# Loading joined with the first similarity, the last similarity begun inside the kernel mix, and rows of inverse lengths moved four at a time

## The chip, the cores and the metric

The kernel runs on one core of a Trainium2 chip. The core has a matrix engine (TensorE, PE in the rows; PEld is its loading of stationary operands), three engines for elementwise work (VectorE, DVE; ScalarE, ACT; GpSimd, POOL), a queue that issues transfers (SyncE, SP) and 16 DMA engines that share them. Each engine runs its own list of instructions in order and waits on semaphores that others raise. The metric is the device time of one execution in microseconds (us), measured over several runs.

## The reference, cut to what matters

`x` is 64 batches of 128 x 512 values, `adj` is 128 x 128. Four layers follow one another, each with a residual sum and a normalisation over the last axis. Layers 0 and 3 are alike and are the ones touched:

```python
def _ada_gcn(xn, weight, bias):             # xn: 512 x 64 x 128
    x_norm = xn / jnp.maximum(jnp.linalg.norm(xn, axis=-1, keepdims=True), 1e-12)
    mean_sim = jnp.einsum('nbl,mbl->nm', x_norm, x_norm) / B
    _, idx = jax.lax.top_k(mean_sim, k + 1)  # k = 153; the row itself is left out
    ...                                      # A: the kept similarities, An: A scaled by its degrees
    xw = jnp.einsum('nbl,lo->nbo', xn, weight)
    return jnp.einsum('sd,sbl->dbl', An, xw) + bias
x = _layernorm(x + _L0_gnn_ref(x, adj, L0_gnn_bias), axis=-1)
x = _layernorm(x + _L1_gnn_ref(...))         # mixes the 128 tokens, adj as kernel
x = _layernorm(x + _L2_gnn_ref(...))         # two causal kernels per batch, made from x
x = _layernorm(x + _L3_gnn_ref(x, adj, L3_gnn_bias), axis=-1)
```

The mean similarity is a sum over all 64 batches of 512 x 512 Gram matrices of columns scaled to length one. So a layer's similarity needs, for every batch, its 512 inverse column lengths, and the choice of neighbours can begin only when all 64 batches are summed.

## The kernel before, in words

All of `x` stays on the chip as `X`, 128 partitions by 64 batches by 512. The stages, each closed by a barrier of all engines, are: `load_x`; `select_neighbours` for layer 0, which is `similarity` and then `neighbours`; `propagate_and_mix_tokens` (layers 0 and 1); `kernel_mix` (layer 2, 16 groups of four batches in a software pipeline); `select_neighbours` for layer 3; `propagate` with the stores of the output.

**Inverse lengths.** In layer 0 ScalarE squares each batch (L448) and TensorE sums the squares over partitions into one row of a bank `rows_bank` (L459). Even and odd batches and the two halves of `x` go to bands of this bank. `ColumnScales` turns the rows into inverse lengths: `clamp` and the maximum (L198, L200), a root on ScalarE, `invert` (L208), `refine` (L213 to L217), and `store` writes them to memory outside the core as `rn_rows` (L222). It exists twice per layer: `early` for the rows that are done when the stage before ends (half of the batches in layer 0, all but the last `LATE` groups in layer 3) and `late` for the others, whose inverse is computed between groups of the similarity.

**Similarity.** For batch b, SyncE brings row b of `rn_rows`, spread over all partitions (256 KB), into slot r = b mod 4 of `rnb` (L514), as soon as the multiply of batch b - 4 has read that slot. VectorE multiplies `X[b]` by it (L576, `unit`), ScalarE makes its 16-bit high part (L617, `hi`), VectorE subtracts to get the low part (L582, `lo`), and TensorE adds 11 products of high and low parts into four banks `pair` and one bank `diag` (L546 to L550). VectorE's list has four multiplies, then four subtractions, per group of four batches; the buffers `unit`, `hi` and `lo` hold four slots each. GpSimd only stores the late rows and takes the greatest of the squared lengths over partitions (L537), which VectorE needs at the end for the scaled weights (L602 to L607). In layer 3, `LastGroup` normalises the last four batches and takes their squares during the first groups.

**Kernel mix.** Step s of the pipeline projects and compares group s, finishes group s - 1 (turned kernels L1748, masks and sums L1913 to L1952, outputs L1979 into `X`, moments, normalising L1819) and takes the squares and sums of group s - 2 (L1803, L2030, L1733). Step 16 has no new group, only what is left of the last two; behind it, `early` of layer 3 stores its rows (L222) and the stage ends.

What sets the order is the order of the code for each engine, written by hand, with semaphore counts between engines.

## Time and profile before

| | |
|---|---|
| median of 3 runs | 1421.34 us (1420.53 to 1422.23) |
| profiled execution | 1420.99 us, its span 1419.3 us |
| mean granted TensorE clock | 0.966 of full speed |
| TensorE busy | 1313.2 us, 93% of the span |
| weight loads (PEld) | 726.5 us, 51% |
| VectorE busy | 1081.6 us, 76% |
| ScalarE busy | 818.8 us, 58% |
| GpSimd busy | 566.3 us, 40% |

The stages in the trace: loading to 60 us, the first similarity to 167.8, neighbours and propagation behind it, the kernel mix to some 1060, the second similarity to 1170, then neighbours, propagation and the stores of the output. A row of the timeline is a run of like instructions: start, time from the first's start to the last's end, engine, line, output and inputs, size, and in brackets how long the engine sat idle before it and what released it. The landing time of a transfer runs from its issue to its last byte.

### The profile page before, as it was taken

To read this page: it belongs to the slowest core of one execution; us is meant where nothing else is said; L and a number is where in the kernel's file an instruction comes from. 1 tells how busy PE (TensorE), PEld (TensorE's weight loads), DVE (VectorE), ACT (ScalarE), POOL (GpSimd) and SP (SyncE) were. 2 spreads that over 40 slices of the span, in tenths; PEclk is the share of its full clock that TensorE was granted. 3 is DMA by queue.
4 is the path that set the end of the run, shared out by engine and by line. 5 is a ranking of instruction groups with operands and counts; after the bars stand their busy time and mean duration, and the time that the engine had idled before them with its cause. 6 is when DMAs were issued, how large, how long until landed. Compare 5 with 4: busy or idle time off the path is not lost. (4 is left out here: it accounts for less than half of the span.)

```text
span 1419.3 us, 29584 instructions
## 1 busy us (share of the span) xinstructions
PE 1313.2 (93%) x8776; PEld 726.5 (51%) x8806; DVE 1081.6 (76%) x2169; ACT 818.8 (58%) x1366; POOL 566.3 (40%) x866
## 2 busy tenths in 40 slices
PE   6689988999999889999999999999947997999997
PEld 2156555555555345555555555555514567455553
DVE  0498777888888847888888888888788988356664
ACT  5634345787777633555555555555445446477776
POOL 2100114787787711222222222222222001688887
PEclk9999987999999889999999999999988998999999
DMA  8756200000000022112211111222205440122222
GB/s 325 266 189 210 89 0 1 1 0 0 0 0 0 12 49 38 38 38 38 38 37 37 37 37 37 43 39 39 36 13 177 161 136 1 45 90 81 81 81 97
DMA packets 122971, 93.62 MB, mean 66 GB/s; under 512 B 87712, under 2 KB 87840, under 8 KB 122912
## 3 DMA queue, kind: packets, MB, share of 16 engines
q1 hardware_dynamic: 122720, 92.81, 22.7%
q8 instruction: 31, 0.51, 0.1%
q14 instruction: 28, 0.23, 0.0%
q0 software_dynamic: 192, 0.08, 0.0%
HBM read 54.86 MB, written 17.04 MB: 51 GB/s over the span
## 5 line engine op out<-in xcount | busy, mean ns | idle before, releaser
L546 PE MATMUL pair<-unit_lo,unit_hi 128*128 128x512 f16 x512 | 178.8, 386 | 29.5 <-ACT unit_hi L617 24.7
L2030 POOL TENSOR_TENSOR sq_lo<-sq,sq_hi 128x512 f16<-128x512 f32 x60 | 69.6, 1160 | 139.2 <-ACT sq_hi L1803 139.2
L550 PE MATMUL diag<-unit_hi 128*128 128x128 f16 x512 | 113.4, 221 | 0.0
L548 PE MATMUL pair<-unit_hi 128*128 128x384 f16 (+2 forms) x384 | 106.4, 277 | 0.0
L1150 PE MATMUL po<-an_h,xwh 128*128 128x512 f16 x256 | 98.0, 383 | 0.0
L1151 PE MATMUL po<-an_l,xwh 128*128 128x512 f16 x256 | 97.9, 382 | 0.0
L1152 PE MATMUL po<-an_h,xwl 128*128 128x512 f16 x256 | 97.8, 382 | 0.0
L1785 PE MATMUL work<-m_h,xT 128*128 128x512 f16 x256 | 97.0, 379 | 0.0
L1786 PE MATMUL work<-m_l,xT 128*128 128x512 f16 x256 | 97.0, 379 | 0.0
L1787 PE MATMUL work<-m_h,xT 128*128 128x512 f16 x256 | 97.0, 379 | 0.0
L1089 POOL TENSOR_TENSOR x_all<-x_all,t 128x512 f32 (+1 forms) x64 | 81.2, 1269 | 16.8 <-ACT t L983 12.1
L2047 POOL TENSOR_TENSOR rnl<-rnl,scalars 128x4 f32<-128x4 f32 x16 | 16.6, 1035 | 176.2 <-DVE rnl L1991 176.2
L1334 POOL TENSOR_TENSOR x_all<-x_all,t 128x512 f32 (+1 forms) x64 | 81.2, 1269 | 9.1 <-ACT t L1235 5.1
L546 PEld LDWEIGHTS pair<-unit_lo,unit_hi 128*128 128x128 f16 x512 | 50.8, 99 | 58.4 <-DVE unit_lo L582 34.0
L550 PEld LDWEIGHTS diag<-unit_hi 128*128 128x128 f16 x512 | 50.9, 99 | 47.2 <-issue 3.3
L617 ACT ACTIVATE unit_hi<-xT 128x512 f16<-128x512 f32 x64 | 39.7, 630 | 60.9 <-DVE xT L576 33.9
L617 ACT ACTIVATE unit_hi<-kept 128x512 f16<-128x512 f32 x64 | 39.3, 628 | 59.6 <-DVE kept L576 37.6
L1870 ACT ACTIVATE v_h<-work 128x512 f16<-128x512 f32 x48 | 28.7, 597 | 77.5 <-PE work L1787 77.5
L1376 PE MATMUL po<-an_h,xwh 128*128 128x512 f16 x184 | 69.7, 379 | 0.0
L1377 PE MATMUL po<-an_l,xwh 128*128 128x512 f16 x184 | 69.7, 379 | 0.0
L1378 PE MATMUL po<-an_h,xwl 128*128 128x512 f16 x184 | 69.7, 379 | 0.0
L1105 POOL TENSOR_TENSOR rstd<-rstd,scalars 128x2 f32<-128x2 f32 (+1 forms) x67 | 65.5, 978 | 10.1 <-POOL rstd L1103 8.6
(438 smaller groups left out, 4237.7 us busy)
## 6 DMA issues: line engine op xcount, KB each, us to landing
x_all<-in_x_dram SPq DMA_DIRECT2D x16, 1024.0 KB, 14.5
tl<-rn_rows SPq DMA_DIRECT2D x64, 256.0 KB, 3.7
sim<-rn_rows SPq DMA_DIRECT2D x64, 256.0 KB, 3.7
out_dram<-x_all SPq DMA_DIRECT2D x64, 256.0 KB, 2.0
weights_a<-in_L_gnn_W_lang_dram SPq DMA_DIRECT2D x1, 1024.0 KB, 11.4
weights_b<-in_L_gnn_W_grav_dram SPq DMA_DIRECT2D x1, 1024.0 KB, 8.3
weights_a<-in_L_gnn_W_O_dram SPq DMA_DIRECT2D x1, 1024.0 KB, 10.6
an_h<-in_L_gnn_W_V_dram SPq DMA_DIRECT2D x1, 512.0 KB, 5.6
```

The source lines that it names most:

```text
L546: nc.tensor.matmul(pair[i][:], stat, lo[:, r, :], start=first, stop=False, skip_group_check=True)
L548: nc.tensor.matmul(pair[i][:, (i + 1) * P:], stat, hi[:, r, (i + 1) * P:], start=False, stop=final, skip_group_check=True)
L550: last = nc.tensor.matmul(diag[:, i * P:(i + 1) * P], stat, stat, start=(first and i == 0), stop=final, skip_group_check=True)
L617: nc.scalar.activation(hi[:, r, :], unit[:, r, :], ACT.Copy).then_inc(hi_ready, 1)
L1089: pool.tensor_tensor(X[:, b, :], X[:, b, :], t[:, r, :], ALU.add).then_inc(add_r, 1)
L1150: nc.tensor.matmul(po[r][:], wh[:, r, cs], an_h[:, c, :], start=(c == 0), stop=False)
L1151: nc.tensor.matmul(po[r][:], wh[:, r, cs], an_l[:, c, :], start=False, stop=False)
L1152: last = nc.tensor.matmul(po[r][:], wl[:, r, cs], an_h[:, c, :], start=False, stop=(c == C - 1))
L1334: pool.tensor_tensor(X[:, b, :], X[:, b, :], t[:, r, :], ALU.add).then_inc(add_r, 1)
L1785: nc.tensor.matmul(work[j][:], xT_h[:, j, d, :], w["m_h"][:, d, :], start=(d == 0), stop=False)
L1786: nc.tensor.matmul(work[j][:], xT_h[:, j, d, :], w["m_l"][:, d, :], start=False, stop=False)
L1787: last = nc.tensor.matmul(work[j][:], xT_l[:, j, d, :], w["m_h"][:, d, :], start=False, stop=(d == C - 1))
```

## The change

- `load_x` and `similarity` of layer 0 become one stage, `load_and_compare`; the barrier between them is gone.
- The similarity of layer 3 is begun in step 16 of the kernel mix (`closing`), whose list for each engine is now written out: groups of the similarity stand between pieces of the mix's last two groups. The clamp, inversion and refinement of the early rows, the first four multiplies and high parts move into step 15. `LATE` goes from 2 to 3 groups. The mix's own banks `work0` to `work3` and `gram_l` are the similarity's `pair` and `diag`; their names stay in the rows.
- One transfer of four rows (1 MB) fills all four slots of the one buffer `rnb`; it is issued when all four multiplies of the group before are done.
- The low parts of slots 1 and 3 are made by GpSimd, in both layers.
- From the seventh sixteenth of `x` on, GpSimd squares one batch in four.
- GpSimd's reduction of the greatest squared length stands at the end of its list, behind its last subtraction. Weight transfers are issued later and in smaller pieces.

```diff
-LATE = 2
+LATE = 3
+class Similarity:
+    R = 4
...
+    def load(self, sp, base):
+        if not isinstance(base, int) or base > 0:
+            settle(sp, self.unit_ready, base, self.k.idle["sp"])
+        row = base if self.layer == 0 else B - self.R - base
+        sp.dma_start(self.rnb, self.k.rn_rows[bass.ds(row, self.R)].partition_broadcast(P)).then_inc(self.rn_in, 16)
...
+    def take_unit(self, dve, base, r, start=False):
+        b = base + r
+        dve.wait_ge(self.rn_in, (base // self.R + 1) * 16)
+        if not start:
+            dve.wait_ge(self.hi_ready, b - self.R + 1)
+            dve.wait_ge(self.lo_of(r), self.lo_count(base - self.R, r))
+        self.k.nc.vector.tensor_tensor(self.unit[:, r, :], self.k.X[:, b, :], self.rnb[:, r, :],
+                                       ALU.mult).then_inc(self.unit_ready, 1)
...
+    def units(self, dve, base, start=False):
+        for r in range(self.R):
+            self.take_unit(dve, base, r, start)
+        for r in range(0, self.R, 2 if self.shared else 1):
+            self.lo_on_vector(dve, base, r, start)
+
+    def lo_on_pool(self, pool, base, start=False):
+        for r in range(1, self.R, 2):
+            b = base + r
+            if not start:
+                settle(pool, self.gram_done, b - self.R + 1, self.k.idle["pool"])
+            settle(pool, self.hi_ready, b + 1, self.k.idle["pool"])
+            pool.tensor_tensor(self.lo[:, r, :], self.unit[:, r, :], self.hi[:, r, :],
+                               ALU.subtract).then_inc(self.lo_of(r), 2 if self.shared else 1)
...
-def load_x(k, x, adj, b0, b3, gate, logsig, mix, rows_bank, tiles, tokens):
+def load_and_compare(k, ctx_out, x, adj, b0, b3, gate, logsig, mix, rows_bank, ops, tokens):
...
                 early.store(sp)
                 early.all_stored(sp)
+                for base in range(0, B // 2, R):
+                    sim.load(sp, base)
+                    if base == 2 * R:
+                        sp.wait_ge(mix.lang.lo_r, C)
+                    if 2 * R <= base < 6 * R:
+                        mix.load_rows(sp, "wo", mix.a, base // R - 2)
+                sim.late.all_stored(sp)
...
                 mix.lang.lo_part(pool, mix.a)
+                for base in range(0, 3 * R, R):
+                    sim.lo_on_pool(pool, base, base == 0)
+                sim.late.store(pool)
+                with strided(pool, 3 * R, B, R) as base:
+                    sim.lo_on_pool(pool, base)
+                pool.wait_ge(early.top, 1)
+                sim.greatest(pool)
...
-def kernel_mix(k, w, rows_bank, head):
+def kernel_mix(k, w, rows_bank, head, work, pgl, pgg, ahead):
...
+                def closing():
+                    early.store(sp)
+                    early.all_stored(sp)
+                    sp.wait_ge(early.top, 1)
+                    for q in range(5):
+                        sim.load(sp, q * R)
+                    turn_kernels(NG - 1)
+                    for q in range(5, (B - LATE * G) // R):
+                        sim.load(sp, q * R)
+                    sim.late.store(sp)
+                    sim.late.all_stored(sp)
+                    for q in range((B - LATE * G) // R, B // R):
+                        sim.load(sp, q * R)
...
+                def closing():
+                    flips(NG - 1)
+                    pe.wait_ge(v_l, NG * G)
+                    pe.wait_ge(ksm, (NG - 1) * SMALL + 1)
+                    for r in range(R):
+                        sim.gram(pe, 0, r, r == 0, False)
...
+                def closing():
+                    ks = Kernels(NG - 1)
+                    for r in range(0, R, 2):
+                        sim.lo_on_vector(dve, 0, r, True)
+                    ks.add_turned()
+                    sim.units(dve, R)
+                    ks.mask_gravity()
+                    ks.sums()
+                    sim.units(dve, 2 * R)
+                    ks.factors()
+                    ks.mix()
...
+                        if before_close(s, 1):
+                            dve.wait_ge(gl_d, NG)
+                            dve.wait_ge(ln_r, (NG - LATE) * G)
+                            for r in range(R):
+                                sim.take_unit(dve, 0, r, True)
```

How the lists change. SyncE where the loading ends and the first similarity begins, before (`tl` is the buffer of the rows of inverse lengths, `an_l` the early inverse lengths):

```order
L222 DMA rn_rows<-an_l 16x512 x2
L394 UNCONDITIONAL_BRANCH
L508 UNCONDITIONAL_BRANCH
L514 DMA tl<-rn_rows 128x512 x4
L352 DMA weights_b<-in_L_gnn_W_grav_dram 128x4x512
L352 DMA weights_a<-in_L_gnn_W_O_dram 128x4x512
L57 UNCONDITIONAL_BRANCH
L57 ISA
L514 ISA
L514 DMA tl<-rn_rows 128x512
```

SyncE at the same place after:

```order
L223 DMA rn_rows<-an_l 16x512 x2
L410 DMA tl<-rn_rows 128x2048 x3
L356 DMA weights_a<-in_L_gnn_W_O_dram 128x512
L410 DMA tl<-rn_rows 128x2048
L356 DMA weights_a<-in_L_gnn_W_O_dram 128x512
L410 DMA tl<-rn_rows 128x2048
L356 DMA weights_a<-in_L_gnn_W_O_dram 128x512
L410 DMA tl<-rn_rows 128x2048
L356 DMA weights_a<-in_L_gnn_W_O_dram 128x512
L410 DMA tl<-rn_rows 128x2048 x2
```

Four row transfers have become one of four rows, the two large weight transfers have left this place, and one of them comes back in quarters.

GpSimd from the end of its weight work to the end of the first similarity, before (`wl_l` is the low part of a weight, L537 the reduction):

```order
L314 TENSOR_TENSOR wl_l<-weights_a,wl_h 128x128
L394 UNCONDITIONAL_BRANCH
L148 ISA
L530 UNCONDITIONAL_BRANCH
L222 DMA rn_rows<-an_l 16x512 x2
L537 ISA
L537 ISA scalars<-scalars 128x1
L507 UNCONDITIONAL_BRANCH
```

GpSimd over the same stretch after (L441 is `lo_on_pool`, L471 the reduction):

```order
L315 TENSOR_TENSOR wl_l<-weights_a,wl_h 128x128
L441 TENSOR_TENSOR unit_lo<-xT_18,unit_hi 128x512 x6
L223 DMA rn_rows<-an_l 16x512 x2
L57 UNCONDITIONAL_BRANCH
L57 ISA
L65 REGISTER_ALU
L441 TENSOR_TENSOR unit_lo<-xT_18,unit_hi 128x512
L65 REGISTER_ALU
L441 TENSOR_TENSOR unit_lo<-xT_18,unit_hi 128x512
L57 REGISTER_ALU
L57 COMPARE_AND_BRANCH
L471 ISA
L471 ISA scalars<-scalars 128x1
```

Two subtractions a group have come to GpSimd, and the reduction has moved from the middle of the stage to behind the loop of them.

VectorE at the end of the kernel mix, before (L1913 to L1932 are masks and sums of the last group):

```order
L1893 SCALAR_TENSOR_TENSOR v_l<-work_288,v_h 128x512
L1913 TENSOR_TENSOR gs<-gs,gram_l 128x512
L1915 TENSOR_TENSOR es<-es,gram_g 128x512
L1917 SCALAR_TENSOR_TENSOR gs<-gs,bcast 128x512
L1924 SCALAR_TENSOR_TENSOR es<-es,mask 128x512
L1930 TENSOR_REDUCE small<-gs 128x4
L1932 TENSOR_REDUCE small<-es 128x4
```

VectorE at the same place after (L418 is the multiply, L426 the subtraction of the similarity; `degrees` here is the bank that was `gram_g`, `diag` the one that was `gram_l`):

```order
L418 TENSOR_TENSOR tl<-x_all,xT_18 128x512 x4
L2014 SCALAR_TENSOR_TENSOR v_l<-work_217,v_h 128x512
L2014 SCALAR_TENSOR_TENSOR v_l<-work_218,v_h 128x512
L2014 SCALAR_TENSOR_TENSOR v_l<-work_219,v_h 128x512
L2014 SCALAR_TENSOR_TENSOR v_l<-work_220,v_h 128x512
L426 TENSOR_TENSOR tg_l<-tl,tg_h 128x512 x2
L2039 TENSOR_TENSOR gs<-gs,diag 128x512
L2041 TENSOR_TENSOR es<-es,degrees 128x512
L2043 SCALAR_TENSOR_TENSOR gs<-gs,bcast 128x512
L418 TENSOR_TENSOR tl<-x_all,xT_18 128x512 x4
L426 TENSOR_TENSOR tg_l<-tl,tg_h 128x512 x2
```

The multiplies of the first batches have come in front of the value parts of the last group, and the second group of the similarity stands between the last group's turned kernels and its sums.

## Rows read from the trace of the kernel before

**Rows 1.** Windows: stretch, length; busy (instructions) PE, PEld, DVE, ACT, POOL; clock, DMA, GB/s

```profile
102.00:166.00 64.00, 63.54 (x496) 38.84 (x494) 54.69 (x91) 26.89 (x44) 0.00 (x0) 1.00 0.56 180
1044.00:1048.00 4.00, 0.00 (x0) 0.00 (x0) 3.83 (x12) 1.44 (x3) 2.27 (x3) 0.52 0.00 0
```

**Rows 2.** Timeline, TensorE and ScalarE: start, length, engine, line, operation [idle before, releaser]

```profile
47.43 12.48 PE L459 MATMUL rows_bank<-sq,unit_col 128*32 128x512 f32 x46
69.72 0.61 PE L546 MATMUL pair<-unit_lo,unit_hi 128*128 128x512 f16 x1 [9.81 <-ACT unit_hi L617]
...
167.78 1.09 ACT L681 ACTIVATE xT<-pair 128x512 f32<-128x512 f32 x2 [4.21 <-PEq L507]
...
1040.26 0.60 PE L1748 MATMUL gram_g<-ident,es 128*128 128x128 f32 x4
1069.94 0.61 PE L546 MATMUL pair<-unit_lo,unit_hi 128*128 128x512 f16 x1 [10.48 <-ACT unit_hi L617]
...
1169.96 1.09 ACT L681 ACTIVATE kept<-pair 128x512 f32<-128x512 f32 x2 [4.21 <-PEq L507]
```

**Rows 3.** Timeline, VectorE, middle of the first similarity

```profile
151.99 2.50 DVE L576 TENSOR_TENSOR xT<-x_all,tl 128x512 f32<-128x512 f32 x4
157.64 2.50 DVE L576 TENSOR_TENSOR xT<-x_all,tl 128x512 f32<-128x512 f32 x4
```

**Rows 4.** Landing times: rows of layer 0 (L514), then parts of x (L400)

```profile
DMA to landing us min/median/max: 3.0/3.7/9.4
...
DMA to landing us min/median/max: 5.2/14.5/16.1
```

**Rows 5.** DMA view and timeline, 0 to 72 us

```profile
GB/s 0 232 379 34 116 313 407 396 387 387 389 387 386 386 390 386 386 383 393 386 385 385 391 387 388 382 391 386 348 161 13 0 0 0 110 341 221 283 385 413
...
tl<-rn_rows SPq DMA_DIRECT2D x8, 256.0 KB, 6.6
...
rn_rows<-an_l SPq DMA_DIRECT2D x2, 32.0 KB, 2.6
...
46.24 12.57 ACT L448 ACTIVATE sq<-x_all 128x512 f32<-128x512 f32 x24
...
51.89 0.82 SPq L222 DMA_DIRECT2D rn_rows<-an_l  x2
...
64.08 2.16 DVE L576 TENSOR_TENSOR xT<-x_all,tl 128x512 f32<-128x512 f32 x3 [9.07 <-DMA tl<-rn_rows]
...
65.01 4.62 SPq L514 DMA_DIRECT2D tl<-rn_rows  x4
```

**Rows 6.** Timeline, a subtraction on GpSimd beside VectorE's multiplies

```profile
1091.31 4.42 DVE L576 TENSOR_TENSOR kept<-x_all,sim 128x512 f32<-128x512 f32 x4
1091.94 3.24 POOL L1532 TENSOR_TENSOR early_xwl<-early_xwh 128x512 f16<-128x512 f32 x2 [7.79 <-ACT early_xwh L1527]
```

**Rows 7.** Timeline: reciprocal of the early rows, the reduction, the weights' chain

```profile
46.37 3.34 DVE L208 RECIPROCAL an_l<-an_h 64x512 f32<-64x512 f32 x1 [4.65 <-ACT an_h L204]
...
98.62 0.47 POOL L537 PARTITION_ALL_REDUCE scalars<-scalars  x1 [7.02 <-issue]
...
163.19 0.15 DVE L602 TENSOR_SCALAR scalars<-scalars 128x1 f32<-128x1 f32 x1
164.16 0.15 DVE L607 TENSOR_SCALAR scalars<-scalars 128x1 f32<-128x1 f32 x1
```

**Rows 8.** Timeline, last step of the mix

```profile
1026.16 2.73 DVE L1979 SCALAR_TENSOR_TENSOR x_all<-work,scalars,x_all 128x512 f32<-128x512 f32 x4 [4.16 <-PE work L1777]
...
1038.96 2.92 ACT L1819 ACTIVATE x_all<-x_all,rs 128x512 f32<-128x512 f32 x4
...
1047.03 1.81 DVE L1947 TENSOR_SCALAR gs<-gs,small 128x128 f32<-128x128 f32 x4
...
1059.06 1.68 SPq L222 DMA_DIRECT2D rn_rows<-xT  x4
```

More of the change, by code:

```diff
@@ L467, in _ @@
                         mix.lang.sum_squares(pe)
+                pe.wait_ge(mix.lang.tmp_r, C)
+                pe.wait_ge(mix.lang.q_in, 1)
+                for r in range(R):
+                    sim.gram(pe, 0, r, r == 0, False)
+                with strided(pe, R, B - R, R) as base:
+                    sim.grams(pe, base)
+                sim.grams(pe, B - R, True)
             @block.vector
@@ L640, in similarity @@
+                sim.units(dve, 0, True)
+                dve.wait_ge(sums, B)
+                sim.late.clamp(dve)
+                sim.units(dve, R)
+                sim.late.invert(dve)
+                sim.units(dve, 2 * R)
+                sim.late.refine(dve)
+                with strided(dve, 3 * R, B, R) as base:
+                    sim.units(dve, base)
+                sim.weights(dve)
     return pair, diag
@@ L1739, in _, with flips, flip @@
                 pe.wait_ge(msk_r, 2)
+                def flips(g):
+                    def flip(bank, src):
+                        for j in range(G):
+                            js = slice(j * P, (j + 1) * P)
+                            end = nc.tensor.transpose(bank[:, js], src[:, js], k.ident[:])
+                        return end
+                    pe.wait_ge(tl_c, g + 1)
+                    pe.wait_ge(diag_r, g * DIAG + 1)
+                    flip(pgl, gs)
+                    need(pe, sum_r, g)
+                    pe.wait_ge(dd_r, g + 1)
+                    nc.tensor.matmul(pbc[:], k.ones[:], dd[:], start=True, stop=True).then_inc(bc_d, 1)
+                    pe.wait_ge(tg_c, g + 1)
+                    flip(pgg, es).then_inc(bc_d, 1)
@@ new lines, in step @@
+                def step(s):
+                    if closes(s):
+                        return closing()
+                    if before_close(s, 1):
+                        dve.wait_ge(ns_d, (NG - LATE) * G)
+                        dve.wait_ge(v_d, (NG - 1) * G)
+                        dve.wait_ge(cleared, 1)
+                        early.clamp(dve)
+                    if s.live(1):
+                        ks = Kernels(s.at(1))
+                        ks.add_turned()
+                    if s.live(0):
+                        for e in range(2):
+                            lo(tl_lo[:, e, :], work[e][:], tl_hi[:, e, :], S_EVAC, tl_h, s.at(0) * C + e + 1, tl_l)
+                    if s.live(1):
+                        ks.mask_gravity()
+                    if s.live(0):
+                        lo(tl_lo[:, 2, :], work[2][:], tl_hi[:, 2, :], S_EVAC, tl_h, s.at(0) * C + 3, tl_l)
+                    if s.live(1):
+                        ks.sums()
+                    if s.live(0):
+                        lo(tl_lo[:, 3, :], work[3][:], tl_hi[:, 3, :], S_EVAC, tl_h, s.at(0) * C + 4, tl_l)
+                    if s.live(1):
+                        ks.factors()
+                        ks.mix()
@@ new lines, in closing @@
+                def closing():
+                    sim.lo_on_pool(pool, 0, True)
+                    mask_language(NG - 1)
+                    last.mark(pool)
+                    for q in range(1, 5):
+                        sim.lo_on_pool(pool, q * R)
+                    scales(NG - 2)
+                    choose(NG - 2)
+                    sim.lo_on_pool(pool, 5 * R)
+                    for j in range(G):
+                        square_lo(NG - 2, j)
+                    sim.lo_on_pool(pool, 6 * R)
+                    last.scales(pool)
+                    sim.lo_on_pool(pool, 7 * R)
+                    last.low_parts(pool)
+                    for q in range(8, B // R):
+                        sim.lo_on_pool(pool, q * R)
+                    sim.greatest(pool)
```

628 lines of the change are left out of this document (332 added, 296 removed).

## The prediction

> **What bounds the kernel now.** I read the page's slices of the span first: TensorE is 93% busy, and its bad slices lie where stages meet. The windows around two of these meetings come next. In the middle of the first similarity TensorE is busy 63.54 of 64.00 us at the full clock; at the end of the mix it does nothing in 1044 to 1048, and the granted clock is down at 0.52 there, the lower level of 1.2 GHz [rows 1]. The timeline gives the size. Join 1: the last square sums end at 59.9, the first Gram matmul starts at 69.72. Join 2: the last turned kernels leave at 1040.86, the first Gram matmul starts at 1069.94; only 12 output products and 8 sums lie between. Behind similarity 1 the next block starts at 167.78, behind similarity 2 at 1169.96, each as soon as TensorE is done [rows 2]. What the change can win is therefore at most some 10 us in join 1 and some 25 in join 2.
>
> In the steady part the four multiplies of one group start 5.65 us after those of the group before (151.99, 157.64) [rows 3]. That is TensorE's pace, 1.41 us a batch, since it never rests there [rows 1]. VectorE spends 2.50 on the multiplies of a group and as much on its low parts, so it has 0.65 us to spare.
>
> **The rows of inverse lengths: the term that decides.** Before, a 256 KB transfer brings one row into one of four slots, and it is issued as soon as that slot's multiply is done. It lands 3.7 us later in the median, 3.0 at best [rows 4]; with a multiply of 0.7 (three in 2.16 [rows 5]) that closes a loop of 4.6 per slot, shorter than 5.65, so it hides. After, one 1 MB transfer fills all four slots, and `load` waits for `unit_ready` of all four. There is no second buffer. So the loop is serial: four multiplies 2.50 [rows 3], the queue's reaction 0.2 (the first multiply of 64.08 is over at 64.80, its reload starts at 65.01) [rows 5], the landing, and 0.1 until VectorE starts.
>
> The landing of 1 MB is not seen alone for these rows; the nearest row is the load of x, same size, whose first transfer found an idle ring: 5.2 us, the least of its 16 [rows 4]. Bounds: 3.7, if size cost nothing, and 6.6, the median landing of the first eight quarter transfers, which shared the ring with 2 MB of weights [rows 5]. I take 5.2. The loop is 2.50 + 0.2 + 5.2 + 0.1 = 8.0 us for four batches instead of 5.65. TensorE then works 5.66 of 8.0 and waits the rest.
>
> The Trainium skill, DMA: Bandwidth & Descriptors, section Anatomy of one DMA, gives about 2.0 us plus bytes over 436 GB/s, which for 1 MB would be 4.4 us. The trace does not quite agree: its 256 KB need 3.0 at best where the rule has 2.6, and the lone 1 MB needed 5.2. By the rule the loop would be 7.2 and the sum near 1439; it is a rival below.
>
> **Half of the low parts on GpSimd.** Two of four subtractions per group leave VectorE (saving 1.2 us) for GpSimd. They don't come free: while GpSimd did two such subtractions in 3.24 us , VectorE's four multiplies took 4.42 instead of 2.50 [rows 3, 6]; I price it at 0.9 us of VectorE per GpSimd subtraction, nothing to 1.0 as bounds. That makes 6 x 0.62 + 2 x 0.9 = 5.5 per group against 5.0 before. In a loop of 8.0 this lies in the landing, so it costs nothing; with the old loop it would have been close to the bound.
>
> **Join 1.** The squares: GpSimd takes one in four from part 6 on, ScalarE's 0.52 per square (24 in 12.57 [rows 5]) was TensorE's wait, so the last 24 take 6 x 0.52 = 3 us less; nothing waits for that but the late rows. The early rows are refined earlier too, but their store stands in the same queue behind x, so I leave it landed at 52.3 + 2.6 = 54.9 [rows 5] (bound: 3 earlier). The load now follows at once, not behind a barrier and beside weights: issued 55.1, landed 60.3, first multiply 60.3 instead of 64.08, first Gram near 64 instead of 69.72. Then 15 loops: 60.3 + 15 x 8.0 = 180.3 for the last group's multiplies; 0.7 more for the 3.34 us reciprocal [rows 7] and the refinement, which stand between groups and mostly fall into landings. From there 2.50 multiplies, 1.1 to the first low parts, 4 x 1.41 Gram: TensorE ends at 190.3.
>
> Then the tail. `greatest`, the reduction over partitions, was done in the middle of the block (7.02 us in which GpSimd waits for no semaphore that the trace shows, then 0.47: 7.5 us) [rows 7]. Now it stands behind GpSimd's last subtraction. That one ends near 181.0 + 5.5; plus 7.5 and VectorE's five small steps, 163.19 to 164.31 or 1.1 [rows 7], gives 195.1, where TensorE was done at 190.3. With 0.3 to the next block: 195.4 against 167.78. **Join 1: +27.6.**
>
> **Join 2.** In step 15 the clamp lies under the turning of the kernels and the reciprocal in VectorE's idle 4.16 us before the outputs [rows 8]; the refinement delays it by about 2, and the moments of step 14 (3.3) have left. So rows are ready near 1029, four stores (1.68 us of issue [rows 8] and 2.6 to land [rows 5]) by 1033.3, the load by 1038.7. VectorE blocks there till its multiplies end at 1041.3, ScalarE puts four high parts between the value copies, and the values are complete near 1044; low parts and the first sum follow, the first Gram starts near 1046, 24 us earlier than now. That is the gain.
>
> The second group's load is issued at 1041.5, multiplies at 1047.2 behind the turned kernels. Then 14 loops of 8.0: 1159.2. VectorE's work of the last step (masks, sums, the 2.9 us of mixing that begins at 1047.03 [rows 8], moments, outputs; 26 us in all) mostly falls into landings. Not all: ScalarE's high parts of group 5 stand behind the normalising of step 14 (2.92 [rows 8]), which waits for GpSimd and the moments, 3.8 late; those of group 7 behind the last group's normalising and squares, 1.8; mixing and reciprocal 1.5; the stores of the late rows between loads 12 and 13, 1.3. Sum 8.4: last multiplies 1167.6, TensorE's end + 9.3 = 1176.9, tail as in join 1 + 4.8, plus 0.9 for three more steps, 0.3: 1182.9 against 1169.96. **Join 2: +12.9**: the 24 won are spent on 14 x 2.35 = 33 of loop.
>
> **Sum.** The profiled execution took 1420.99 us (span 1419.3; the median of the runs, 1421.34, is 0.35 above it). 1420.99 + 27.6 + 12.9 = 1461.5, so about **1462**, slower.
>
> **Rivals.**
> (a) The rule's landing of 4.4, loop 7.2: 15 x 0.8 and 14 x 0.8 less, 12.0 + 11.2, of which VectorE's crowded closing takes back some: near 1439. For it: the ring moved 385 to 413 GB/s through the load of x [rows 5], so a megabyte needs 2.7 of transfer, and a group's four rows are 8 KB in one piece. Against: the lone megabyte took 5.2. 0.22.
> (b) Loop longer than 8: GpSimd's subtractions meet the multiplies, or TensorE, idle a third of each loop, falls to the low clock. In join 2 the clock was down within 3 to 7 us after TensorE's last turn at 1040.86 [rows 1, 2]; the gaps here are 2.4. One more us of loop is 29 us: about 1490. 0.12.
> (c) The other side: faster. If a megabyte lands in 3.7 like a quarter of it, the loop is 6.5. Join 1 then costs 27.6 - 22.5 - 1.5 (first load) = 3.6; join 2, there bound by VectorE at (16 x 5.5 + 26) / 16 = 7.1 a group, wins 12.9 - 14 x 0.9 - 1.5 - 6 (ScalarE's late parts no longer the wait) = -7. Near 1418. It decides from a loop of about 6.6 down. Against it: 1 MB in the 1.4 us that a landing of 3.7 leaves is 750 GB/s, twice what x's load got [rows 5]. 0.07.
> (d) The joins don't overlap as told (a wait in step 15 that I missed holds the first Gram beyond 1050): 1470, inside the forecast's range.
> Forecast 0.59, with its own range 1450 to 1476.
>
> A measurement of this kernel tells 0.2%, some 3 us, from no change. Faster 0.06, same 0.03, slower 0.91. Range 1435 to 1484: it leaves out (c), half of (b) and the low edge of (a).
>
> **What would show it.** In the profile after: multiplies of one group start 7.5 to 8.5 us after the last group's, with VectorE's idle before them ended by the DMA of the rows; landings of these 1 MB transfers near 5.2; TensorE busy about 0.7 in both similarities at clock 1.00; first Gram near 64 and 24 us earlier in join 2; GpSimd idle 7 us before the reduction at each block's end, and VectorE waiting for it. I am wrong if the groups keep 5.7, if landings are below 4, or if the similarities are bound by VectorE or GpSimd rather than by the rows.

## The result, and the profile after

The changed kernel takes 1459.82 us in the median of four runs (1459.64 to 1463.21) against 1420.93 of before in the same session: ratio 1.028, 95% interval 1.0268 to 1.0293. It is slower by 39 us. Its profiled span is 1461.5 us against 1419.3.

| | before | after |
|---|---|---|
| span of the profiled execution | 1419.3 | 1461.5 |
| TensorE busy | 1313.2 (93%) | 1329.4 (91%) |
| VectorE busy | 1081.6 (76%) | 1089.4 (75%) |
| GpSimd busy | 566.3 (40%) | 666.1 (46%) |
| clock | 0.966 | 0.96 |

The middle of the first similarity, the stretch of [rows 1], in the windows after (same columns):

```profile
102.00:166.00 64.00, 47.25 (x358) 27.59 (x356) 47.33 (x51) 20.10 (x34) 25.09 (x18) 1.00 0.48 168
```

TensorE issues 358 matmuls where it issued 496, at the same clock, and is idle a quarter of the time. VectorE's timeline at the place of [rows 3], then SyncE's, then the landing times of the transfers of layer 0 and of layer 3 (from issue to last byte):

```profile
146.03 2.50 DVE L418 TENSOR_TENSOR xT<-x_all,tl 128x512 f32<-128x512 f32 x4 [2.14 <-DMA tl<-rn_rows]
148.44 3.20 DVE L426 TENSOR_TENSOR unit_lo<-xT,unit_hi 128x512 f16<-128x512 f32 x2
153.80 2.50 DVE L418 TENSOR_TENSOR xT<-x_all,tl 128x512 f32<-128x512 f32 x4 [2.16 <-DMA tl<-rn_rows]
...
148.75 8.12 SPq L410 DMA_DIRECT2D tl<-rn_rows  x2
...
DMA to landing us min/median/max: 4.1/4.7/5.0
...
DMA to landing us min/median/max: 4.2/4.7/5.7
```

Read it as one circle. The multiplies end at 148.53, the transfer is issued at 148.75, the next multiplies start at 153.80: 2.50 + 0.22 + 5.05 = 7.77 us, where [rows 3] had 5.65. Of the 5.05, the landing of this transfer is 4.7, and some 0.35 pass from it to the first multiply. What ends VectorE's idle time is the transfer.

The end of each similarity, on GpSimd and VectorE, with TensorE's last matmul of the second:

```profile
179.09 2.86 POOL L441 TENSOR_TENSOR unit_lo<-xT,unit_hi 128x512 f16<-128x512 f32 x2 [3.75 <-ACT unit_hi L449]
187.81 0.38 POOL L471 PARTITION_ALL_REDUCE scalars<-scalars  x1 [5.85 <-issue]
188.22 0.15 DVE L477 TENSOR_SCALAR scalars<-scalars 128x1 f32<-128x1 f32 x1 [5.71 <-POOL scalars L471]
...
1203.07 0.22 PE L461 MATMUL diag<-tg_h 128*128 128x128 f16 x1
...
1205.22 0.38 POOL L471 PARTITION_ALL_REDUCE scalars<-scalars  x1 [6.20 <-issue]
1205.63 0.15 DVE L477 TENSOR_SCALAR scalars<-scalars 128x1 f32<-128x1 f32 x1 [7.63 <-POOL scalars L471]
1209.03 2.04 PE L1622 MATMUL rows_bank<-adj_scaled,x_all 128*128 128x128 f32 x8 [5.74 <-PEq L151]
```

GpSimd needs 6 us before its reduction in which it waits for no semaphore that the trace shows (5.85 and 6.20), VectorE waits for it, and TensorE stands from 1203.3 to 1209.0. In layer 0 TensorE's last Gram product ends at 186.8 and the next block starts at 189.8; before, 0.3 us lay between in both layers. TensorE's granted clock is lower in the first 5 us of the next block. Windows of before (two), then of after (two):

```profile
167.80:172.80 5.00, 2.64 (x20) 2.17 (x21) 4.10 (x9) 1.07 (x2) 1.67 (x18) 1.00 0.00 2
1170.00:1175.00 5.00, 3.77 (x28) 3.11 (x29) 4.11 (x9) 1.64 (x3) 1.59 (x18) 1.00 0.02 3
```

```profile
189.80:194.80 5.00, 3.45 (x14) 2.66 (x15) 3.59 (x8) 1.08 (x2) 1.15 (x17) 0.57 0.00 0
1209.00:1214.00 5.00, 4.87 (x20) 4.10 (x20) 3.19 (x6) 1.68 (x3) 1.14 (x17) 0.50 0.00 0
```

The granted clock was 1.00 there before and is 0.57 and 0.50 now. 0.50 is the lower of its two levels; 0.57 means that it lay there for most of the window. In layer 0, 14 matmuls take 3.45 us where 20 took 2.64. The price can be read on equal work, from the first copy of the block to the first use of its threshold (the line that is L691 before): 10.99 us against 9.45 in layer 0, 9.78 against 8.35 in layer 3.

**Where the time went.** Four marks stand in both kernels: the first copy of `neighbours` in each layer (the line that is L681 before), the first product of the first propagation (L1150 before) and the end. The stretches between them, for every kernel of this study:

| us | load and similarity 0 | neighbours 0 | propagation to end of similarity 3 | rest | span |
|---|---|---|---|---|---|
| before | 167.8 | 56.1 | 946.1 | 249.3 | 1419.3 |
| after | 189.8 | 58.0 | 961.2 | 252.5 | 1461.5 |
| per_row | 167.6 | 57.7 | 948.3 | 250.7 | 1424.4 |
| two_rows | 174.8 | 58.0 | 953.8 | 251.0 | 1437.6 |
| per_row_vec | 164.8 | 57.3 | 944.8 | 251.0 | 1417.9 |
| before_4row | 191.9 | 56.9 | 967.2 | 249.4 | 1465.4 |
| two_buffers | 187.8 | 57.2 | 945.9 | 250.6 | 1441.6 |
| after_vec | 185.5 | 57.1 | 952.0 | 250.8 | 1445.4 |
| per_row_l0vec | 162.2 | 57.3 | 949.1 | 252.4 | 1421.0 |
| early_reduction | 198.2 | 57.5 | 964.0 | 250.5 | 1470.2 |
| reordered | 163.8 | 56.7 | 937.9 | 251.5 | 1409.9 |
| reordered_again | 163.3 | 57.5 | 937.6 | 249.9 | 1408.3 |
| reordered_share4 | 163.1 | 56.9 | 936.8 | 250.1 | 1406.9 |

The change costs 22.0 in the first stretch, 1.9 in the second, 15.1 in the third and 3.2 in the last.

Each row is one profiled execution. `reordered` and `reordered_again` are the same kernel and differ by 0.3 to 1.6 us in the four stretches; `per_row_vec`, `per_row_l0vec` and `reordered` are the same up to the end of layer 0 and differ by 2.6 us in the first. So a difference of 1 or 2 us in one stretch says little by itself.

### The profile page after: what moved, and what is told of

Its sections match the earlier page's. It is cut to its first block and busy times, and to the rows that moved or that the text cites. A ratio compares the mean times of both kernels' runs of the same rounds, so it can differ in the third digit from the quotient of the medians.

```text
span 1461.5 us, 28809 instructions
## 1 busy us (share of the span) xinstructions
PE 1329.4 (91%) x8776; PEld 734.2 (50%) x8806; DVE 1089.4 (75%) x2105; ACT 815.1 (56%) x1358; POOL 666.1 (46%) x936
## 5 line engine op out<-in xcount | busy, mean ns | idle before, releaser
L457 PE MATMUL pair<-unit_lo,unit_hi 128*128 128x512 f16 x256 | 92.0, 392 | 29.6 <-DVE unit_lo L426 29.5
L457 PE MATMUL work<-tg_l,tg_h 128*128 128x512 f16 x256 | 94.4, 401 | 26.6 <-DVE tg_l L426 19.9
L1114 POOL TENSOR_TENSOR x_all<-x_all,t 128x512 f32 (+1 forms) x64 | 81.3, 1270 | 15.7 <-ACT t L1008 11.8
L441 POOL TENSOR_TENSOR unit_lo<-xT,unit_hi 128x512 f16<-128x512 f32 x32 | 44.4, 1403 | 70.5 <-ACT unit_hi L449 70.5
L441 POOL TENSOR_TENSOR tg_l<-tl,tg_h 128x512 f16<-128x512 f32 x32 | 46.2, 1453 | 63.9 <-ACT tg_h L449 63.9
L449 ACT ACTIVATE tg_h<-tl 128x512 f16<-128x512 f32 x64 | 38.7, 627 | 55.6 <-DVE tl L418 45.3
L2014 DVE SCALAR_TENSOR_TENSOR tl<-work,tl 128x512 f16<-128x512 f32 x64 | 42.6, 686 | 31.9 <-ACT tl L1883 31.7
## 6 DMA issues: line engine op xcount, KB each, us to landing
x_all<-in_x_dram SPq DMA_DIRECT2D x16, 1024.0 KB, 14.4
```

The source lines that it names most:

```text
L441: pool.tensor_tensor(self.lo[:, r, :], self.unit[:, r, :], self.hi[:, r, :], ALU.subtract).then_inc(self.lo_of(r), 2 if self.shared else 1)
L457: nc.tensor.matmul(pair[i][:], stat, lo[:, r, :], start=first, stop=False, skip_group_check=True)
```

## The experiments

**Rows of inverse lengths one to a transfer** (per_row). The edit to the changed kernel:

```diff
-        if not isinstance(base, int) or base > 0:
-            settle(sp, self.unit_ready, base, self.k.idle["sp"])
-        row = base if self.layer == 0 else B - self.R - base
-        sp.dma_start(self.rnb, self.k.rn_rows[bass.ds(row, self.R)].partition_broadcast(P)).then_inc(self.rn_in, 16)
+        for r in range(self.R):
+            if not isinstance(base, int) or base > 0:
+                settle(sp, self.unit_ready, base - self.R + r + 1, self.k.idle["sp"])
+            row = (base if self.layer == 0 else B - self.R - base) + r
+            sp.dma_start(self.rnb[:, r, :], self.k.rn_rows[row].partition_broadcast(P)).then_inc(self.rn_in[r], 16)
```

> The changed kernel, but each row of inverse lengths is again its own 256 KB transfer into its slot, issued once that slot's multiply is done; both joins, GpSimd's subtractions and the late reduction stay. Theory (the serial loop of the 1 MB transfer costs the time): groups of the first similarity start 5.7 to 6.1 us apart instead of 7.76, VectorE's idle before the multiplies is gone, the first similarity ends 25 to 28 us earlier, the second 20 to 30 us earlier: 1400 to 1415 us, faster than before by 5 to 20. Rival 1 (the loop is long because GpSimd's subtractions slow VectorE): groups stay above 7 us apart and the time above 1440. Rival 2 (the joins themselves cost): near 1421 or above even with a loop of 5.7.

Measured: 1428.28 us, ratio to before 1.0053 (1.0036 to 1.0069). 31.5 us come back, and the last groups of the first similarity are 5.7 us apart again (146.63 to 152.30). Over all 15 groups the mean is 6.2, as in the kernel before (6.24), not 5.7. The time is 13 above the upper end of what was expected and near the figure of rival 2, the joins themselves: with the loop gone the kernel is still slower than before, so something else in the change costs at least as much as both joins win. This run does not say what; `per_row_vec` does.

**Four rows to a transfer in the kernel before** (before_4row). The same loop without any join:

```diff
-                    for r in range(R):
-                        load(base + r, r)
+                    load(base)
...
+                def load(base):
+                    if not isinstance(base, int) or base > 0:
+                        settle(sp, unit_ready, base, k.idle["sp"])
+                    row = base if layer == 0 else B - R - base
+                    sp.dma_start(rnb[:], k.rn_rows[bass.ds(row, R)].partition_broadcast(P)).then_inc(rn_in, 16)
```

> The kernel before, with only the rows of inverse lengths changed: one 1 MB transfer of four rows per group, waited for as in the changed kernel. No join, no work moved to GpSimd. Theory (serial loop): groups 7.7 to 7.8 us apart in both similarities, 2.1 us more than 5.65 for each of 15 groups in each layer, 63 us in all, less what the pieces of VectorE's work between groups take back in layer 3: 1475 to 1485 us. Rival 1 (GpSimd's subtractions make the loop long): groups below 6.5 us, under 1440. Rival 2 (the transfer hides here since VectorE's low parts all stand on VectorE and fill the landing): near 1425.

Measured: 1468.64 us, 1.0341 (1.0318 to 1.0365). Groups start 7.79 us apart in layer 0 (65.74 to 182.60 for 15) and 7.70 in layer 3, with no subtraction on GpSimd: both rivals fall. The result is 6 us below the lower end of what was expected, for a plain reason: before, the 15 groups of layer 0 took 93.56 us from the first multiply to the last (64.08 to 157.64), 6.24 each and not 5.65, since some early groups come later: one stands behind VectorE's reciprocal of 3.35 us, and in the first two VectorE waits 2.13 and 1.57 us for rows while the weights are being loaded. The loop costs 24.1 and 21.1 us in the two layers.

**Two rows to a transfer** (two_rows). The changed kernel with two transfers of 512 KB a group.

```diff
+        for h in range(2):
+            if not isinstance(base, int) or base > 0:
+                settle(sp, self.unit_ready, base - self.R + 2 * h + 2, self.k.idle["sp"])
+            row = (base if self.layer == 0 else B - self.R - base) + 2 * h
+            sp.dma_start(self.rnb[:, 2 * h:2 * h + 2, :],
+                         self.k.rn_rows[bass.ds(row, 2)].partition_broadcast(P)).then_inc(self.rn_in[h], 16)
```

> The changed kernel, but two rows (512 KB) come to a transfer: slots 0 and 1 in one, slots 2 and 3 in another, each issued once its own two multiplies are done. Theory (what counts is that the next load can start while the other slots are still in use): two multiplies 1.25, queue 0.2, landing about 3.6 to 4.0 (between 3.7 of 256 KB and 4.7 of 1 MB, measured), so 5.1 to 5.6 per half, below or at the pace of 5.7 to 6: 1400 to 1420, within 8 us of one row to a transfer. Rival (large transfers as such slow the core, by ring or memory traffic): half way between the changed kernel and one row each, 1430 to 1440.

Measured: 1438.97 us, 1.0118 (1.0101 to 1.0135), 11 above per_row: outside the 8 expected, and at the rival's figure. Its landings, and VectorE's timeline in the middle and near the end of the first similarity:

```profile
DMA to landing us min/median/max: 3.4/3.9/6.8
...
133.81 1.39 DVE L420 TENSOR_TENSOR xT<-x_all,tl 128x512 f32<-128x512 f32 x2 [0.85 <-DMA tl<-rn_rows]
137.14 1.50 DVE L420 TENSOR_TENSOR xT<-x_all,tl 128x512 f32<-128x512 f32 x2 [1.95 <-DMA tl<-rn_rows]
138.56 1.28 DVE L428 TENSOR_TENSOR unit_lo<-xT,unit_hi 128x512 f16<-128x512 f32 x2
141.09 1.29 DVE L420 TENSOR_TENSOR xT<-x_all,tl 128x512 f32<-128x512 f32 x2 [1.26 <-DMA tl<-rn_rows]
...
155.93 2.25 DVE L420 TENSOR_TENSOR xT<-x_all,tl 128x512 f32<-128x512 f32 x2 [0.79 <-DMA tl<-rn_rows]
...
162.26 2.25 DVE L420 TENSOR_TENSOR xT<-x_all,tl 128x512 f32<-128x512 f32 x2 [0.70 <-DMA tl<-rn_rows]
```

The median landing, 3.9, is what was expected. What the expectation missed is the multiplies: beside GpSimd's subtractions two of them take 2.25 us where it counted 1.25. The circle at the end is then 2.25 for the multiplies, 0.2 for the queue, 3.5 for the landing of the transfer issued at 158.4 and some 0.35 to the next multiply, 6.3 us, and that is the distance from 155.93 to 162.26. So a circle above the pace explains these groups without the rival's slower core; a run of this kernel without GpSimd's share, which would settle it, was not made.

**A second buffer for the megabyte** (two_buffers): before_4row with a second `rnb` in layer 3 alone, loops unrolled.

```diff
-                    if not isinstance(base, int) or base > 0:
-                        settle(sp, unit_ready, base, k.idle["sp"])
+                    ahead_by = R if layer == 3 else 0
+                    if base > ahead_by:
+                        settle(sp, unit_ready, base - ahead_by, k.idle["sp"])
...
-                    sp.dma_start(rnb[:], k.rn_rows[bass.ds(row, R)].partition_broadcast(P)).then_inc(rn_in, 16)
+                    sp.dma_start(rnbs[base // R % 2][:], k.rn_rows[bass.ds(row, R)].partition_broadcast(P)).then_inc(rn_in[base // R % 2], 16)
```

> The kernel before with 1 MB transfers of four rows, as in the second experiment, but in layer 3 alone a second buffer of four rows, so that the load of a group is issued while the multiplies of the group before have still to run; layer 0 keeps one buffer. (The loops over groups are unrolled.) Theory (the landing of the megabyte costs only because nothing can be issued before all four slots are free): layer 3 goes back to 5.65 us a group and loses its 21 us, layer 0 keeps its 24: 1445 to 1450 us. Rival (a megabyte in one transfer is slow or disturbs the core whatever the buffers): layer 3 stays above 7 us a group, 1460 to 1470.

Measured: 1441.02 us, 1.0125 (1.0108 to 1.0142). The third stretch is 945.9 against 967.2 with one buffer and 946.1 before: all of the loop's cost in layer 3 is gone, with the same megabyte in one transfer. The unrolled loops are no rival for it: layer 0 has them too, kept one buffer, and kept a loop above 7 us. So the cause is the circle through the single buffer, and not the size of the transfer. Layer 0 gained 4 us that were not expected: its groups came 7.36 us apart (68.16 to 178.51) instead of 7.79; unrolled loops and a second load issued ahead of the weights are both in that, and they were not told apart.

**GpSimd's half taken away** (per_row_vec, after_vec, per_row_l0vec). `shared` is False, all low parts are VectorE's, and the reduction stands early:

```diff
-        sim = Similarity(k, rows_bank, 1.0, 0, (pair, diag), (ops.sim, ops.kept, hi, lo), tiles, True)
+        sim = Similarity(k, rows_bank, 1.0, 0, (pair, diag), (ops.sim, ops.kept, hi, lo), tiles, False)
...
-                for base in range(0, 3 * R, R):
-                    sim.lo_on_pool(pool, base, base == 0)
                 sim.late.store(pool)
-                with strided(pool, 3 * R, B, R) as base:
-                    sim.lo_on_pool(pool, base)
                 pool.wait_ge(early.top, 1)
                 sim.greatest(pool)
```

Layer 3 has the like edit in `closing`. The first of them on top of per_row, in both layers:

> One row to a transfer, both joins, but all low parts on VectorE and so GpSimd's reduction of the greatest squared length early in the list, as before the change. Theory: without GpSimd beside it VectorE needs 5.0 us a group, so the first similarity goes at TensorE's 5.65 a group and its end does not wait for the reduction: 2 to 5 us earlier there than with GpSimd's share. In the second similarity VectorE has all low parts beside 26 us of the mix, (16 x 5.0 + 26) against 16 x 5.7 + 26 with slowed multiplies, so it too gains or is level: 1395 to 1408. Rival (GpSimd's share is worth having: VectorE is the bound in the second similarity and 32 subtractions of 0.62 come back onto it): 5 to 20 us slower than with the share, 1415 to 1430.

Measured: 1416.19 us, 0.9953 (0.9937 to 0.997): 12 us below per_row and 0.5% faster than before. It missed its range of 1395 to 1408, which had been built on the too low figure for per_row. The second, on the changed kernel with its megabytes:

> The changed kernel with its 1 MB transfers and single buffer, but all low parts on VectorE and the reduction of the greatest squared length early, as before the change. Theory (the loop is the landing's, GpSimd's share lies in it; what the share costs is the end of each similarity, where the reduction is late, TensorE idles and its clock falls): groups stay 7.7 to 7.8 us apart; the next block begins 2 to 3 us earlier in both layers, and finds TensorE's granted clock at 1.00 instead of 0.57 and 0.50, which gives 2 us in the first block of neighbours and 3 behind the second: 1447 to 1453 us. Rival (the share also relieves VectorE in the mix's closing): what is won at the ends is lost there, 1456 to 1462.

Measured: 1447.12 us, 1.0175 (1.0157 to 1.0192), 12.7 below the changed kernel and just at the lower end of what was expected. Between the two profiled executions it is 16.1 us: by the table 4.3 in the first stretch, 0.9 in the second, 9.2 in the third and 1.7 in the last. TensorE's list shows where they arise. From its last Gram product to the next block it stands 0.3 us in layer 0 (185.16 to 185.46) where `after` has 3.0 (186.83 to 189.85), and 1.2 us in layer 3 (1193.35 to 1194.56) where `after` has 5.7 (1203.29 to 1209.01). These waits for the late reduction are 7.2 of the 16.1; 2.6 lie behind the two similarities; the other 6.3 are in the groups, 1.7 in layer 0 and 4.7 in layer 3 with the mix's closing. In layer 0 the last multiplies start at 176.16 instead of 176.88, so there the share itself did lie in the landing. The first 5 us of its two blocks of neighbours are again at a clock of 1.00 (windows, columns as above):

```profile
185.50:190.50 5.00, 2.67 (x20) 2.19 (x21) 4.11 (x9) 1.05 (x2) 1.60 (x18) 1.00 0.00 0
1194.60:1199.60 5.00, 3.77 (x28) 3.11 (x29) 4.11 (x9) 1.64 (x3) 1.59 (x18) 1.00 0.00 0
```

The third, with GpSimd's half in layer 3 alone:

> One row to a transfer and both joins, with all low parts on VectorE and the reduction early in layer 0 only; in layer 3 GpSimd keeps its half and the late reduction. It splits the 12 us between the two kernels with one row to a transfer. Theory (the share costs by GpSimd working beside VectorE's multiplies and by the late reduction, in each layer alike): layer 0 ends like the one with all low parts on VectorE (next block at 165 instead of 168), layer 3 like the one with shares: 1422 to 1426 us. Rival (only layer 3, where ScalarE's late high parts meet GpSimd's waits, pays): 1427 or above; or only layer 0: 1417.

Measured: 1421.84 us, 0.9996 (0.9987 to 1.0006), about half of the 12 us for each layer, at the lower edge of the theory's range. Subtractions that run beside the multiplies slow both, as the timeline of VectorE and GpSimd of per_row, and of VectorE of per_row_vec, shows:

```profile
117.71 3.45 DVE L419 TENSOR_TENSOR xT<-x_all,tl 128x512 f32<-128x512 f32 x4
121.08 0.68 DVE L427 TENSOR_TENSOR unit_lo<-xT,unit_hi 128x512 f16<-128x512 f32 x1
122.49 0.83 DVE L427 TENSOR_TENSOR unit_lo<-xT,unit_hi 128x512 f16<-128x512 f32 x1 [0.73 <-ACT unit_hi L450]
...
117.89 1.50 POOL L442 TENSOR_TENSOR unit_lo<-xT,unit_hi 128x512 f16<-128x512 f32 x1 [1.26 <-ACT unit_hi L450]
```

```profile
119.23 2.50 DVE L419 TENSOR_TENSOR xT<-x_all,tl 128x512 f32<-128x512 f32 x4
121.64 1.89 DVE L427 TENSOR_TENSOR unit_lo<-xT,unit_hi 128x512 f16<-128x512 f32 x3
124.17 0.69 DVE L427 TENSOR_TENSOR unit_lo<-xT,unit_hi 128x512 f16<-128x512 f32 x1 [0.64 <-ACT unit_hi L450]
```

Beside one subtraction of GpSimd four multiplies take 3.45 instead of 2.50, and GpSimd's own 1.50 (1.15 when alone). VectorE was spared 0.62.

But with one row to a transfer this is not what the share costs. TensorE's last Gram product of layer 0 ends at 163.40 in per_row, at 164.49 in per_row_vec and at 161.85 in per_row_l0vec; in layer 3 it ends 942.0, 943.6 and 943.1 us behind the first product of the first propagation. The groups are not slower with the share than without it. What differs is the wait behind them: 4.2 us with the late reduction against 0.3 in layer 0, 6.3 (per_row) and 6.1 (per_row_l0vec) against 1.2 in layer 3. So what the traces show of the 12 us is the reduction, which the share pushes to the end of GpSimd's list. They do not show all of it: the profiled executions of per_row and per_row_vec differ by 6.5 us only.

**Only the reduction moved** (early_reduction). The changed kernel with:

```diff
                 sim.late.store(pool)
+                pool.wait_ge(early.top, 1)
+                sim.greatest(pool)
                 with strided(pool, 3 * R, B, R) as base:
                     sim.lo_on_pool(pool, base)
-                pool.wait_ge(early.top, 1)
-                sim.greatest(pool)
```

and in layer 3 `greatest` behind the low parts of group 11.

> The changed kernel (1 MB transfers, GpSimd's half of the low parts) with only GpSimd's reduction moved: in layer 0 behind the store of the late rows, in layer 3 behind the low parts of group 11. Theory (the late reduction holds TensorE at each end, and its clock falls for the block behind): the next block begins 2.5 to 3 us (layer 0) and 5 us (layer 3) sooner after the last Gram matmul, at a granted clock of 1.00, which shortens what follows by 2 and 3; against it GpSimd's 6 to 7 us of code loading delays one group in each layer by 2 to 3 us: 1450 to 1454. Rival (the stall in the middle costs as much as the end gains): 1457 to 1462.

Measured: 1470.72 us, 1.0339 (1.0321 to 1.0357), 11 slower than the changed kernel where 6 to 10 faster were expected. GpSimd's timeline shows why:

```profile
94.48 0.38 POOL L471 PARTITION_ALL_REDUCE scalars<-scalars  x1 [7.05 <-issue]
101.94 2.26 POOL L441 TENSOR_TENSOR unit_lo<-xT,unit_hi 128x512 f16<-128x512 f32 x2 [7.09 <-issue]
```

GpSimd stands 7.05 us before the reduction and 7.09 more before the next ordinary subtraction, so 14.5 us for one reduction, and VectorE waited 9.34 us for the low part. At the ends the waits went as the theory had it: from the last multiplies to the next block it is 10.2 us instead of 13.0 in layer 0 and 11.2 instead of 15.7 in layer 3, and the clock behind layer 3 is 1.00 again. Behind layer 0 it is not: the first 5 us have a granted clock of 0.79, though TensorE's idle time there is the same 1.67 us as in the kernel before, and 0.81 in reordered_again, where reordered, the same kernel, has 1.00. So the low clock at that place has a second cause, which stays open. Neither of the two places tried for the reduction beside a share of the loop was cheap.

**ScalarE's order in the closing** (reordered): per_row_vec with

```diff
                     hi(4)
-                    normalise(NG - 2)
-                    square(NG - 2, 0)
                     hi(5)
-                    for j in range(1, G):
+                    normalise(NG - 2)
+                    for j in range(G):
                         square(NG - 2, j)
                     hi(6)
+                    hi(7)
                     last.normalise(act)
...
                     last.squares(act, range(0, 2))
-                    hi(7)
-                    last.squares(act, range(2, G))
                     hi(8)
+                    last.squares(act, range(2, G))
                     hi(9)
```

> One row to a transfer, both joins, low parts on VectorE, early reduction, and in ScalarE's list of the mix's closing the high parts of group 5 stand ahead of the normalising of the last but one group, those of group 7 ahead of the last group's normalising (the squares move with them). In the run without this VectorE sat idle 5.2 and 6.3 us waiting for those high parts, and TensorE with it at half clock. Theory: most of these 11.5 us come back, less what VectorE then waits for elsewhere: 1406 to 1411 us. Rival (the work behind then waits for the later squares and the late rows, so the stall only moves): 1414 to 1418.

Measured: 1409.04 us, 0.9905 (0.9888 to 0.9921), 7 below per_row_vec, all in the third stretch, and inside the range expected. VectorE's wait in per_row_vec, and the same stretch of both in the windows (columns as in [rows 1]; per_row_vec first):

```profile
1081.70 3.10 DVE L427 TENSOR_TENSOR tg_l<-tl,tg_h 128x512 f16<-128x512 f32 x4 [5.21 <-ACT tg_h L450]
...
1076.00:1082.00 6.00, 1.96 (x13) 0.76 (x9) 0.79 (x2) 4.92 (x8) 1.57 (x5) 0.89 0.51 167
```

```profile
1076.00:1082.00 6.00, 4.20 (x28) 2.20 (x28) 5.71 (x12) 4.48 (x8) 1.28 (x2) 1.00 0.27 101
```

**A share where GpSimd is idle** (reordered_share4, beside reordered_again): GpSimd takes two low parts of groups 1 to 4 of layer 3 alone.

```diff
+        given = self.shared and isinstance(base, int) and self.R <= base <= 4 * self.R
+        for r in range(0, self.R, 2 if given else 1):
```

> The fastest kernel so far once more, beside the next one: 1407 to 1411 us.

> The fastest kernel so far, but in the mix's closing GpSimd makes two of four low parts of groups 1 to 4, where the trace shows it nearly idle and VectorE 99% busy. VectorE is spared 8 subtractions of 0.62, 5.0 us. Theory (a GpSimd subtraction takes about 0.9 us from VectorE's instructions beside it, as 3.45 us against 2.50 for four multiplies showed): no gain, 0 to 3 us slower, 1409 to 1413. Rival (only the multiplies are slowed and the low parts lie elsewhere): 3 to 5 us faster, 1404 to 1406.

Measured: 1408.56 (0.9903, 0.9886 to 0.9921) and 1407.36 us (0.9895, 0.9879 to 0.9912). The second lies between what the theory and the rival expected. The two intervals overlap for the most part: no difference that these runs can tell. Both are some 15 us below before, the fastest of the study.

## Why the prediction was right, and where it was not

The forecast of 1462 is 2 us from the 1459.82 measured. The mechanism stands: before_4row makes the loop without a join or a share, and two_buffers takes it away with the same megabyte. That the sum came so near is in part luck. Its terms were off by 5.6 us too much in join 1, 2.2 too little in join 2 and 5.1 that were not in it, and most of that cancels. (The terms are read from the profiled execution, which took 1463.21.)

- **The loop** was forecast at 8.0 us and is 7.77. The landing is 4.7 us in the median, between the 5.2 that I took [rows 4] and the 4.4 of rival (a); multiplies and queue were as forecast, and the 0.1 from landing to multiply is some 0.35. In the middle of the first similarity TensorE is busy 0.74, the clock is 1.00 and VectorE's idle time is ended by the transfer, as told. The Trainium skill (DMA: Bandwidth & Descriptors, Anatomy of one DMA) has its 2.0 us plus bytes over 436 GB/s for transfers that GpSimd issues; these are issued by SyncE, which the prediction did not say. Estimated by that rule 256 KB, 512 KB and 1 MB take 2.6, 3.2 and 4.4 us. The trace does not agree: medians of 3.7, 3.9 and 4.7, so the base is higher and the step from size to size smaller.
- **What the loop cost** was put too high. The prediction set 2.35 us a group against a pace of 5.65, 33 us in layer 3. Against the real kernel before, whose groups of layer 0 take 6.24 in the mean, before_4row shows 24.1 and 21.1 us.
- **Join 1** was forecast at +27.6 and is +22.0. Of the 5.6 too much, 3.5 are the loop (15 groups: 60.42 to 176.88 is 116.5 instead of 120), 0.7 the reciprocal that hid, 1.4 the tail (13.0 from the last multiplies to the next block, not 14.4: GpSimd's last subtraction was done at 181.95 and the reduction took 6.2 instead of 7.5). The first Gram product came at 65.64 (forecast near 64); the first multiplies took 3.40 beside GpSimd's low parts of the weights (58.74 to 62.67).
- **Join 2** was forecast at +12.9 and is +15.1. Its first Gram product is at 1069.0, which less the 24.0 us that the kernel was late by then is 1045.0: forecast 1046, 24.9 us before [rows 2]. The last multiplies are at 1193.34, 1169.4 less that shift (forecast 1167.6). One sign did not hold: the clock was forecast at 1.00 in both similarities, and in layer 3 it is 0.88 from 1070 to 1145, beside the closing of the mix, and 0.97 from there to 1195.
- **Not forecast at all** were the 1.9 and 3.2 us behind the two similarities. I named the late reduction and the wait of TensorE for it, and stopped there; behind that wait the granted clock was 0.57 and 0.50, and the block paid 1.5 and 1.4 us by the equal work above. With the wait gone in after_vec the clock is 1.00 in both blocks and the 1.5 and 1.4 are gone. In layer 3 this holds for every kernel: 9.8 us for that work in the four with a late reduction, 8.4 in all others. In layer 0 the low clock also came twice without the wait (0.79 and 0.81 above). The rest of the last stretch, some 1.7 us, differs by as much between two executions of one kernel and stays open.
- **GpSimd's share** was put at nothing, since in a loop of 8.0 it lies in the landing. For the steady groups of layer 0 that is right (0.7 us at the last multiplies). What was missing is the rest: of the 16 us between after and after_vec some 6 are in the groups, most of them in layer 3 with the mix's closing, which is not in a landing. The late reduction was priced, at 4.8 us of TensorE's wait in each layer, and costs 2.7 and 4.5. The contention was read right (0.9 us a subtraction, [rows 6]; 0.95 is measured), and it lengthens the circle of two_rows; with one row to a transfer no run shows that it costs time.
- **The joins** are worth what per_row_vec and reordered show: the first takes 3 to 6 us from the first stretch when GpSimd has no share in it (162.2 to 164.8 against 167.8). The second starts the Gram products 24 us earlier, but only 1.3 us of it remain in per_row_vec, and 8.2 once two waits for ScalarE are taken out. VectorE is busy 9.7 to 9.9 of 10 us in three windows of the closing of reordered, and may hold the rest; that was not tested. What the second join alone would give in the old order was not tried.
- **Rivals.** (a), 1439, fell, though the landing was half way to it. (b) fell: no slower loop, and in after no low clock in the middle of the first similarity; before_4row and after_vec have 0.95 there, with the same loop. (c) fell: the landing is 1.0 us above that of a quarter. Of (d) nothing is seen.

## What to carry to other kernels

A transfer made larger saves issues, but it also ties its buffers together: with one buffer the loop becomes work plus landing, whatever is idle. Before merging transfers, add up that circle and compare it with the pace. When it is longer, either a second buffer or smaller transfers, each issued as soon as its own slot is free, take the cost away; in layer 3 of this kernel both gave the same time. Work given to an engine that looks idle can push that engine's other duties to a worse place: here the two subtractions a group hardly cost in the steady loop, and the reduction behind them held TensorE at the end of each similarity. After such a wait look at the granted clock of the next block too; here 3.0 and 5.7 us of waiting were followed by some 1.5 us more each.

## What the runs showed of the hardware

- GpSimd's reduction over partitions is paid on both sides when ordinary work stands around it: 7.05 us before it and 7.09 us before the next subtraction; the reduction itself is 0.38 (early_reduction, layer 0).
- Rows spread over 128 partitions land in 3.0, 3.4 and 4.1 us at best for 256 KB, 512 KB and 1 MB: four times the bytes cost 1.1 us more. With one buffer the next multiplies waited for the whole landing, with two they did not (before_4row, two_buffers).
- One GpSimd subtraction of 1.50 us lengthens VectorE's four multiplies from 2.50 to 3.45 (per_row).
- In layer 3 the granted clock of the first 5 us behind the similarity was 0.50 after TensorE had stood 5.7 us (after), and 1.00 after it had stood 1.2 us (after_vec); equal work took 9.78 and 8.37 us.
